# Cross attention over the queries: the softmax sums read one slot later, and the placed queries written by ScalarE instead of GpSimd

## The reference

```
q = x @ Wq + bq                      # 16 heads of 8
k = ctx @ Wk + bk;  v = k            # the values are the keys
p = softmax(q k^T / sqrt(8))         # per head, over the 64 context tokens
x = layernorm(x + (p v) @ Wo + bo)
```

## Time and profile before

| | us |
|---|---|
| median of three runs | 1647.3 |
| the profiled execution | 1648.98 |
| its span in the trace | 1647.2 |
| the cross stage, first `mx` to last `pe_in` | 509.3 to 787.3 |
| VectorE busy, whole span | 1224.6 (74%) |
| TensorE busy | 1347.4 (82%) |
| ScalarE busy | 1013.7 (62%) |
| GpSimd busy | 770.0 (47%) |

### The profile page before, as it was taken

How to read it: one execution, slowest core, us unless ns; L and a number is a source line. 1 busy time by engine, 2 the same in 40 slices (tenths; PEclk the granted TensorE clock), 3 DMA queues, 4 the chain that set the end, 5 groups by cost and what they waited for, 6 DMA issues and landing times.

```text
span 1647.2 us, 62636 instructions
## 1 busy us (share of the span) xinstructions
PE 1347.4 (82%) x26438; PEld 878.2 (53%) x26438; DVE 1224.6 (74%) x2581; ACT 1013.7 (62%) x1749; POOL 770.0 (47%) x1535
## 2 busy tenths in 40 slices
PE   5788888888867676776677779999999998998897
PEld 2445545555543443444344446666666666666685
DVE  2445655666455887888788869989989999999856
ACT  2465666776644554454566667777777777777645
POOL 2334544455435778777667653433443332332133
PEclk9799999999876888887555569999999999999979
DMA  7000000000000000000000000000000000000012
GB/s 197 2 3 2 3 3 3 3 3 3 2 2 20 16 16 17 20 16 16 1 1 1 1 1 3 3 3 3 3 3 10 16 16 22 16 16 16 3 34 70
DMA packets 28664, 24.22 MB, mean 15 GB/s; under 512 B 3676, under 2 KB 23906, under 8 KB 28386
## 3 DMA queue, kind: packets, MB, share of 16 engines
q1 hardware_dynamic: 28386, 20.21, 4.5%
HBM read 15.94 MB, written 4.19 MB: 12 GB/s over the span
## 4 chain that ended last, share of the span: by engine, by line
PE 36%; issue 22%; ACT 18%; POOL 16%; DVE 7%; SPq 0%; DMA 0%; POOLq 0%; ACTq 0%; DVEq 0%
PE keys_T L577 7%; ACT keys_pexp L662 5%; POOL gla_low L1108 4%; PE keys_E L473 3%; POOL gla_yg L1132 3%; ACT ffn_hqT L1825 3%; DVE cross_mx L338 2%; ACT keys_pT L644 2%; ACT xs L305 2%; PE keys_E L516 2%; PE ffn_OUT L1786 2%; POOL gla_sq L1125 2%; PE cross_O L875 2%; PE keys_O L584 2%; PE keys_S L319 1%
## 5 line engine op out<-in xcount | busy, mean ns | idle before, releaser
L644 ACT ACTIVATE keys_pT<-keys_T 128x512 f32<-128x512 f32 x256 | 152.5, 596 | 107.5 <-PE keys_T L577 104.2
L328 POOL TENSOR_SCALAR keys_spread<-keys_kT,keys_heads 128x512 f32<-128x512 f32 x128 | 86.9, 697 | 259.4 <-ACT keys_kT L608 259.4
L338 DVE TENSOR_REDUCE keys_mx<-keys_S 128x16 f32<-128x1024 f32 x128 | 156.6, 1223 | 38.5 <-PE keys_S L543 23.5
L577 PE MATMUL keys_T<-ident_sb,keys_pexp 128*128 128x128 f32 x1024 | 165.0, 284 | 22.5 <-ACT keys_pexp L662 18.5
L577 PEld LDWEIGHTS keys_T<-ident_sb,keys_pexp 128*128 128x128 f32 x1024 | 112.8, 141 | 97.9 <-ACT keys_pexp L662 50.5
L341 DVE TENSOR_TENSOR keys_pe_in<-keys_S,keys_mx 128x1024 f32<-128x1024 f32 x128 | 156.7, 1224 | 4.4
L1519 DVE COPY_PREDICATED gla_at<-gla_node,gla_GP 128x256 f32<-128x256 int32 x128 | 64.8, 506 | 97.0 <-ACT gla_at L1393 93.6
L662 ACT ACTIVATE keys_pexp<-keys_pe_in 128x1024 f32<-128x1024 f32 x128 | 134.1, 1048 | 0.2 <-DVE keys_pe_in L341 0.2
L697 DVE RECIPROCAL keys_rinv<-keys_O 128x128 f32<-128x128 f32 x128 | 120.4, 941 | 0.0
L945 ACT ACTIVATE cross_pexp<-cross_pe_in 128x1024 f32<-128x1024 f32 x64 | 67.4, 1053 | 69.2 <-DVE cross_pe_in L341 69.0
L1108 POOL TENSOR_TENSOR gla_low<-gla_ex,gla_kT 128x128 f32<-128x128 f32 x160 | 72.0, 482 | 70.8 <-ACT gla_ex L1384 70.8
(11 more groups left out here) (281 smaller groups left out, 3663.6 us busy)
## 6 DMA issues: line engine op xcount, KB each, us to landing
context<-in_ctx_T SPq DMA_DIRECT2D x32, 256.0 KB, 2.7
xs<-in_x SPq DMA_DIRECT2D x8, 512.0 KB, 7.4
out_x<-xs SPq DMA_DIRECT2D x16, 256.0 KB, 2.3
keys_mask_q<-keys_mask_b SPq DMA_DIRECT2D x64, 1.0 KB
keys_bias_right_f<-in_alibi_right SPq DMA_DIRECT2D x1, 512.0 KB, 3.9
ffn_w<-in_L_ffn_w_gate_T SPq DMA_DIRECT2D x1, 256.0 KB, 4.8
ffn_w<-in_L_ffn_w_up_T SPq DMA_DIRECT2D x1, 256.0 KB, 5.0
ffn_w<-in_L_ffn_w_down_T SPq DMA_DIRECT2D x1, 256.0 KB, 5.6
```

The costliest lines, as they stand in the source:

```text
L328: nc.gpsimd.tensor_scalar(spread[:, :, :, j, :].rearrange("q t s k -> q (t s) k"), flat.rearrange("q (a k) -> q a k", k=SEQ), heads[:, j:j ...
L338: nc.vector.tensor_reduce(m, quads(S), X, ALU.max).then_inc(c["mx"], 1)
L577: last = nc.tensor.transpose(T[:, j * P:(j + 1) * P], pexp[:, t % 2, (4 * half + j) * P:(4 * half + j + 1) * P], sh.ident[:, :])
L644: nc.scalar.activation(pT[:, t % 2, 4 * half:4 * half + 4, :].rearrange("q n k -> q (n k)"), T[:, :], ACT.Copy).then_inc(c["pT"], 1)
```

## The change

- ScalarE writes `spread` itself: instead of one `qT` copy in part 1 it runs four copies (two in part 1, two in part 2), each `Identity` with scale and bias taken from a column of `scale_heads` and `bias_heads`, which are zero outside the rows of head j. The buffer `qT`, its semaphore and GpSimd's four operations per group are gone. TensorE's key projection waits for all four copies where it waited for `qT`.
- The lags grow by one tile: `sums` and `rinv` are of tile n-2, `vz` and `weigh` of tile n-3, `oT`, `output`, residual and moments of tile n-4, the normalisation of tile n-8. `pairs` and `exp` keep theirs.
- The stage drains its tail in the first slots of the ffn stage with two tail slots in the second of them (`drained`, `rush=1`).

```diff
+    def drained(self, n):
+        if self.rush is None or n < self.rush:
+            return range(n, min(n + 1, self.lag))
+        if n == self.rush:
+            return range(n, min(n + 2, self.lag))
+        return range(n + 1, min(n + 2, self.lag))
...
-                if before and n < before.lag:
-                    before.slot(before.groups * G + n)
+                if before:
+                    for k in before.drained(n):
+                        before.slot(before.groups * G + k)
...  gpsimd
-                if part == 2:
-                    c.await_nth(pool, "qT", g, 1, 1)
-                    c.free_tile(pool, "scores", g, G - 1)
-                    pool_spread(nc, pool, c, spread[:, p, :, :, :, :], qT[:, p, :], heads)
...
-                if n := back(g, p, t, 2):
+                if n := back(g, p, t, 3):
                     scale_values(*n)
...
-                if (n := back(g, p, t, 3)) and n[2] == G - 1:
+                if (n := back(g, p, t, 4)) and n[2] == G - 1:
                     pool_moments(nc, pool, sh, b, c, n[0], n[1])
...  tensor
-                    c.await_nth(pe, "qT", g, 1, 1)
+                    c.await_nth(pe, "spread", g, QH, QH)
                     pe.wait_ge(c[f"ctx{p}"], (g - p) * 8 + 16)
                     project(wk, cT[:, p, :], "k_done")
...
-                if n := back(g, p, t, 3):
+                if n := back(g, p, t, 4):
                     output(*n)
...
-                if n := back(g, p, t, 2):
+                if n := back(g, p, t, 3):
                     weigh(*n)
...  scalar
-                if part == 1:
-                    c.await_nth(act, "q_done", g, 1, 1)
-                    c.free_group(act, "spread", g, QH)
-                    nc.scalar.activation(qT[:, p, :], E_[:, :], ACT.Identity, bias=bq[:, 0:1], scale=qscale[:, 0:1]) \
-                        .then_inc(c["qT"], 1)
+                if part in (1, 2):
+                    if part == 1:
+                        c.await_nth(act, "q_done", g, 1, 1)
+                        c.free_tile(act, "scores", g, G - 1)
+                    for j in (2 * part - 2, 2 * part - 1):
+                        nc.scalar.activation(spread[:, p, :, :, j, :].rearrange("q t s k -> q (t s) k"),
+                                             E_[:, :].rearrange("q (a k) -> q a k", k=SEQ), ACT.Identity,
+                                             bias=bias_heads[:, j:j + 1], scale=scale_heads[:, j:j + 1]) \
+                            .then_inc(c["spread"], 1)
...  vector
+                    nc.vector.tensor_scalar(scale_heads[:, :], heads[:, :], float(1 / np.sqrt(8.0)), None, ALU.mult) \
+                        .then_inc(c["prep"], 1)
+                    nc.vector.tensor_scalar(bias_heads[:, :], scale_heads[:, :], bq[:, 0:1], None, ALU.mult) \
+                        .then_inc(c["prep"], 1)
...
-                if n := back(g, p, t, 1):
+                if n := back(g, p, t, 2):
                     invert_sums(*n)
```

More of the change, by code:

```diff
@@ L122, with __init__ @@
 class Part:
-    def __init__(self, early=None, halves=(), lag=0, parts=2 * G, groups=NG, body=None, prepare=None):
-        self.early, self.halves, self.lag, self.parts = early, halves, lag, parts
+    def __init__(self, early=None, halves=(), lag=0, parts=2 * G, groups=NG, body=None, prepare=None, rush=None):
+        self.early, self.halves, self.lag, self.parts, self.rush = early, halves, lag, parts, rush
         self.groups, self.body, self.prepare = groups, body, prepare or (lambda stage, g: None)
@@ L733, in attention_over_queries @@
         bq, bk, bo = kept("bq", [P, 1]), kept("bk", [P, 1]), kept("bo", [P, D])
-        heads, qscale = kept("heads", [P, QH]), kept("qscale", [P, 1])
+        heads = kept("heads", [P, QH])
+        scale_heads, bias_heads = kept("scale_heads", [P, QH]), kept("bias_heads", [P, QH])
         cT = sh.cT
@@ L737, in attention_over_queries @@
         b.xT = sb("xT", [P, 2, GW])
-        kT, qT = sb("kT", [P, 2, GW]), sb("qT", [P, 2, GW])
+        kT = sb("kT", [P, 2, GW])
         spread = sb("spread", [P, 2, G, 2, QH, SEQ])
@@ L756, in attention_over_queries @@
         c.new(*NORM_SEMS, "weights", "zeros", "prep", "ctx0", "ctx1", "xr", "xT_done", "xT", "k_done", "kT",
-              "q_done", "qT", "spread", "v_done", "v", "scores", "mx", "sub", "exp", "paired", "sums", "rinv", "vz",
+              "q_done", "spread", "v_done", "v", "scores", "mx", "sub", "exp", "paired", "sums", "rinv", "vz",
               "pv", "oT")
@@ L818, in rest @@
             def rest(g, p, t):
-                if (n := back(g, p, t, 3)) and n[2] == G - 1:
+                if (n := back(g, p, t, 4)) and n[2] == G - 1:
                     pool_moments(nc, pool, sh, b, c, n[0], n[1])
-            return Part(early, (halve, rest), 3)
+            return Part(early, (halve, rest), 4, rush=1)
         @stage.on("tensor")
@@ L891, in first @@
                     scores(*n)
-                if n := back(g, p, t, 3):
+                if n := back(g, p, t, 4):
                     output(*n)
             def second(g, p, t):
-                if n := back(g, p, t, 2):
+                if n := back(g, p, t, 3):
                     weigh(*n)
-            return Part(early, (first, second), 3)
+            return Part(early, (first, second), 4, rush=1)
         @stage.on("scalar")
@@ L935, in second @@
             def second(g, p, t):
-                if n := back(g, p, t, 7):
+                if n := back(g, p, t, 8):
                     scalar_normalise(nc, act, sh, b, c, *n)
@@ L945, in second @@
                     nc.scalar.activation(pexp[:, tt, :], pe_in[:, tt % 2, :], ACT.Exp).then_inc(c["exp"], 1)
-            return Part(early, (first, second), 7)
+            return Part(early, (first, second), 8, rush=1)
         @stage.on("vector")
@@ L953, in prepare @@
                     dve.wait_ge(c["weights"], NW)
-                    nc.vector.memset(qscale[:, :], float(1 / np.sqrt(8.0))).then_inc(c["prep"], 1)
+                    nc.vector.tensor_scalar(scale_heads[:, :], heads[:, :], float(1 / np.sqrt(8.0)), None, ALU.mult) \
+                        .then_inc(c["prep"], 1)
                     dve.wait_ge(c["prep"], 1)
-                    nc.vector.tensor_scalar(bq[:, :], bq[:, :], qscale[:, 0:1], None, ALU.mult).then_inc(c["prep"], 1)
+                    nc.vector.tensor_scalar(bias_heads[:, :], scale_heads[:, :], bq[:, 0:1], None, ALU.mult) \
+                        .then_inc(c["prep"], 1)
             def invert_sums(g, p, t):
@@ L974, in slot @@
                     vector_residual(nc, dve, sh, b, c, gg, p2, tt, OUT[:, tt * D:(tt + 1) * D])
-                if n := back(g, p, t, 1):
+                if n := back(g, p, t, 2):
                     invert_sums(*n)
-            return Part(lambda g, p, part: None, (lambda g, p, t: None, slot), 3, prepare=prepare)
+            return Part(lambda g, p, part: None, (lambda g, p, t: None, slot), 4, prepare=prepare, rush=1)
         return stage
```

## The result

The changed kernel took 1695.2 us (median of 4 runs, 1691.1 to 1696.8) against 1646.2 us (4 runs) for the kernel before on the same chip: ratio 1.027, 95% interval 1.024 to 1.031. A second comparison, on other executions, gave 1702.2 against 1656.1, ratio 1.030 (1.025 to 1.034). The ratios are estimated from undisturbed runs alone and need not equal the quotient of the two medians. The prediction had the sign, and both places of the loss, but 1668 us with a range to 1690. The measured time is nearest to what its rival 3 described (1703 us).

A forecast was written before the change was run, and what follows sets the result against it. VectorE's waits for pairs and scores, 1.81 us a regular group, were taken as the loss. Terms 11.1 + 6.8 + 2.0 + 1.2 = 21.1 us on 1648.98, with the median 1.7 lower, gave 1668 us, range 1650 to 1690.

The forecast's parts named there:

- rival 3: Lower clock throughout the chain, both projections behind a wait: +56 us, 1703 us; chance 0.09.
- Which wait goes: VectorE's sums, now of tile n-2, no longer wait 1.30 us for GpSimd's pairs.
- What takes its place: Moments delay vz and weigh of slot 0; slot 0 then waits 2.6 us, +11.1 us over 14 group boundaries.
- The copies: ScalarE's four copies, 0.68 us between starts, delay the key projection in slot 1: +6.8 us over 15 groups.
- the first group's 2.0 us: In the first group nothing covers the copies; the key projection starts three times 0.68 later, +2.0 us.
- I take 3.3, since that very place showed it: Chain from slot 0's weigh through query projection and scores to the next maximum, priced at the 3.34 us measured before.
- the forecast's own bound at the lower level: The same weigh-to-maximum chain wholly at the lower clock: 4.3 us, giving +25 us at the group boundaries.
- the copies' 0.45 in slot 1: Key projection waits for the fourth copy, so slot 1's wait is 0.45 us, +6.8 us over 15 groups.
- The end of the stage: One more weigh of 1.18 us lies in the drain: +1.2 us, bounds 0 to 3.
- 1 and 2: Rivals: clock holds, 1658.6 us, chance 0.20; nothing measurable, clock holds and copies start 0.50 apart, 1651 us, chance 0.14.
- 4: Rival: faster, if slot 0's vz starts before 1.1 us after its mx; 1632 or 1639 us, chance 0.09.
- the forecast's bound at the full clock: Lower bound of the +11.1 us for the moments at the group boundaries: +1.3 us.

The follow-up runs named there:

- all fills: Changed kernel plus overwritten TensorE products: four ahead of the output product in slots 2 and 3, eight ahead of slot 0's weigh; 1662.7 us, ratio 1.006.
- moved moments and fills in slots 2 and 3: Changed kernel with moments behind slot 0's vz and pairs, normalisation of tile n-9, four added products each in slots 2 and 3; 1654.5 us, ratio 1.000.

## Why the prediction was wrong

- *Which wait goes.* The wait of `sums` for `pairs` went, in every group. Right.
- *What takes its place.* The moments hold `vz` of slot 0 and through it the query projection and scores of slot 1. Right, with its times to 0.04 us (2.53 for 2.56, 2.99 for 3.03); the lag alone shows it without the copies, and moving the moments removes it.
- *The copies.* Their price (0.67 each for 0.68) and the first group's 2.0 us: right. Their place: right to 0.02 us where TensorE is at the full level (with all fills); in the changed kernel the key projection starts at T + 2.35 for 2.33 by luck, since `weigh` at the lower level ends last there and the copies are through 0.5 us earlier than forecast. Alone they add 8.5 us to the stage where 6.8 was forecast.
- *What failed: the term "I take 3.3, since that very place showed it".* The chain from `weigh` to the maximum was mis-sized. The measured one is 4.38, the forecast's own bound at the lower level (4.3). The second term, the copies' 0.45 in slot 1, was mis-sized in the same way: it was priced with the key projection at the full level, and that projection is at the lower one. With both at the lower level slot 0's wait is 3.5 and slot 1's 1.7, where I added 2.6 and 0.45. The waits add up to 71.4 us where before they were 32.3, 39 us more; the forecast's two terms were 11.1 + 6.8 = 18. These 21 us are most of the 27 by which the forecast was short; the other 6 or so lie outside the stage and stay open. The sum at the lower bound of the clock was 1703, and its chance was put at 0.09. The clock of before was read as a fixed property of the place, and it is not: the same chain ran at the lower level throughout in the changed order. The fills show that it is the level, and not the two places, that was mis-sized: with them the same order gives the full level's waits. Why this order keeps the level down for longer stays open. It is not more idle time, which is 4.8 us a group for 4.7, in shorter stretches; that filling the stretches brings the level back is shown, which of their lengths and places the level answers to is not.
- *The Trainium skill.* TensorE: Matmul & The Clock Gate, Part 1, says that the throttled state is the default and activity releases it. That was cited as speaking for the upper bound, and the runs agree in direction: more work on TensorE, granted clock 0.68 to 0.99. The premise put beside it, that TensorE's idle time per group grows, did not come true (4.7 and 4.8 us).
- *The end of the stage.* +1.2 was forecast; between the last `mx` and the keys stage nothing changed (196.7 and 196.9). Drawing two tail slots together cost no more than before.
- *Rivals.* 1 and 2 needed a clock that holds, 4 needed `vz` before T + 1.1; it came at 2.53. Rival 3 is what happened. The argument against it, that the level came back within 3.3 us each time, was read from one group and does not hold for the kernel before either: there the level was down from 716.1 to 722.9 us, and in the changed kernel for 13.6 us. A small slip without effect: by its own rows the forecast's bound at the full clock is 3.03 + 2.64 - 3.73 - 1.81 = 0.13 a group, +1.8 and not +1.3.

## What to carry to other kernels

When a change moves a wait on TensorE, price everything behind it at both clock levels, and treat the level as an outcome of the change. Adding up TensorE's idle time does not foretell it (4.7 and 4.8 us a group here, at clocks of 0.83 and 0.68 in the stage); a run with added products in the idle stretches shows what the level costs. When a pipeline's lag grows, look at what moves along on each engine: here ten small operations of GpSimd moved by one slot into the one place that had a projection behind it. Where a value is needed soon and a chain that nobody waits for stands ahead of it, put the chain behind. Added products are not free: where the level has already fallen they run at it, and what stands behind them waits.

## What was not expected of the hardware

- The lower level came without a long idle stretch: in the changed kernel it fell between 736 and 737 us, in slot 3, after stretches of 0.88, 1.05 and 0.81 us, and in the same group it had stayed low until 729.8 although TensorE was busy for all but 0.6 us of 720.1 to 729.8.
- The order of the work alone does not fix it: the same order of instructions in a group takes 15.8 or 17.1 us in the kernel with moved moments and fills in slots 2 and 3.
- Products that nobody reads made the changed kernel faster: 16 more in every group, and a ratio of 1.006 instead of 1.03.
